# A hybrid SSM, attention and expert kernel: three PSUM banks for the up products and one for the attention

## The reference, cut to what matters

```
x = x + ssm(layernorm(x))        # scan over the tokens, 64 channels x 8 states
x = x + ffn(layernorm(x))        # 8 experts of 512, all computed, weighed by a router
x = x + attention(layernorm(x))  # 16 heads of 8; windows of 10 tokens with 25 to the left
x = x + ffn(layernorm(x))

g = einsum('bsh,ehf->ebsf', x, w_gate);  u = einsum('bsh,ehf->ebsf', x, w_up)
h = silu(g) * u
out = einsum('ebsh,bse->bsh', einsum('ebsf,efh->ebsh', h, w_down), cw)
```

## Time and profile before

| | |
|---|---|
| median of 3 runs | 1531.04 us (1530.69 to 1531.13) |
| the profiled execution | 1530.76 us, its span 1529.0 us |
| TensorE, its weight loads | 94%, 82% of the span |
| VectorE, ScalarE, GpSimd | 62%, 51%, 33% |
| granted TensorE clock, mean | 0.984 |

### The profile page before, as it was taken

How to read it: one execution, slowest core, us unless ns; L and a number is a source line. 1 busy time by engine, 2 the same in 40 slices (tenths; PEclk the granted TensorE clock), 3 DMA queues, 4 the chain that set the end, 5 groups by cost and what they waited for, 6 DMA issues and landing times.

```text
span 1529.0 us, 31357 instructions
## 1 busy us (share of the span) xinstructions
PE 1442.1 (94%) x12756; PEld 1247.8 (82%) x12756; DVE 946.7 (62%) x2125; ACT 772.8 (51%) x1037; POOL 503.1 (33%) x446
## 2 busy tenths in 40 slices
PE   5788889999999999999999989999999999999998
PEld 3677767888878878888888778888888888888887
DVE  5645558665766757666676566757765566575543
ACT  6453726654457444654546465455643554355321
POOL 5241344323432354135520373117511421241000
PEclk9999999999999999999999999999999999999999
DMA  5110151004201330024001510042004200420000
GB/s 184 33 48 23 45 143 32 19 27 131 40 2 41 105 81 2 9 89 116 14 2 39 134 43 13 1 136 57 29 2 118 40 2 1 118 40 1 2 7 8
DMA packets 82092, 75.50 MB, mean 49 GB/s; under 512 B 4748, under 2 KB 60076, under 8 KB 81948
## 3 DMA queue, kind: packets, MB, share of 16 engines
q1 hardware_dynamic: 74444, 58.58, 14.7%
q10 hardware_dynamic: 7504, 14.91, 2.7%
HBM read 60.65 MB, written 12.83 MB: 48 GB/s over the span
## 4 chain that ended last, share of the span: by engine, by line
PE 71%; DVE 9%; DMA 6%; ACT 5%; issue 5%; POOL 3%; SPq 1%; ACTq 0%; DVEq 0%; POOLq 0%
PE pd L1001 23%; PE pg L272 7%; PE pu L272 6%; PE pg L274 6%; PE pg L273 6%; PE pu L273 6%; PE pu L274 6%; DMA arena<-bc_spread 3%; PE att_ps L678 3%; DVE h L1094 2%; PE att_ps L700 2%; PE att_ps L705 1%; POOL arena L628 1%; DVE ffn_rows L295 1%; DMA qk_rows<-qk_parts 1%
## 5 line engine op out<-in xcount | busy, mean ns | idle before, releaser
L1056 ACT ACTIVATE h<-pg 128x512 f32<-128x512 f32 x512 | 303.4, 597 | 693.7 <-PE pg L274 687.5
L1001 PEld LDWEIGHTS pd<-w_down,h 128*128 128x128 f32 x4096 | 517.4, 194 | 31.9 <-issue 2.5
L1001 PE MATMUL pd<-w_down,h 128*128 128x128 f32 x4096 | 530.1, 278 | 0.8 <-DVE x L1082 0.8
L1094 DVE TENSOR_TENSOR h<-h,pu 128x512 f32<-128x512 f32 x512 | 345.6, 679 | 222.4 <-PE pu L274 220.7
L272 PE MATMUL pg<-ffn_x_hi,w_gate_hi 128*128 128x512 f32 x512 | 246.3, 481 | 1.5 <-DVE ffn_x_lo L355 1.5
L272 PE MATMUL pu<-ffn_x_hi,w_up_hi 128*128 128x512 f32 x512 | 207.0, 404 | 25.1 <-DVE h L1094 24.7
L273 PE MATMUL pg<-ffn_x_lo,w_gate_hi 128*128 128x512 f32 x512 | 204.6, 400 | 0.0
L274 PE MATMUL pg<-ffn_x_hi,w_gate_lo 128*128 128x512 f32 x512 | 204.4, 399 | 0.0
L273 PE MATMUL pu<-ffn_x_lo,w_up_hi 128*128 128x512 f32 x512 | 204.3, 399 | 0.0
L274 PE MATMUL pu<-ffn_x_hi,w_up_lo 128*128 128x512 f32 x512 | 204.2, 399 | 0.0
L903 POOL TENSOR_TENSOR att_arena<-att_arena 128x512 f32<-128x512 f32 (+1 forms) x72 | 72.8, 1011 | 349.4 <-DVE att_arena L775 349.2
(11 more groups left out here) (192 smaller groups left out, 1539.2 us busy)
## 6 DMA issues: line engine op xcount, KB each, us to landing
arena<-bc_spread ACTq DMA_DIRECT2D x56, 256.0 KB
att_arena<-v_rows SPq DMA_DIRECT2D x64, 144.0 KB, 3.9
qk_rows<-qk_parts SPq DMA_DIRECT2D x32, 256.0 KB, 3.1
q<-qk_rows SPq DMA_DIRECT2D x32, 256.0 KB, 3.7
k<-qk_rows SPq DMA_DIRECT2D x32, 256.0 KB, 4.5
att_arena<-v_rows SPq DMA_DIRECT2D x64, 128.0 KB, 3.6
arena<-in_x SPq DMA_DIRECT2D x8, 256.0 KB, 2.8
x<-in_x SPq DMA_DIRECT2D x8, 256.0 KB, 3.5
```

The costliest lines, as they stand in the source:

```text
L1001: last = nc.tensor.matmul(pd[:, t * P:(t + 1) * P], h_b[:, d % NH, t * P:(t + 1) * P], wd[:, d % NCH, :], start=d % CPE == 0 and t == 0, s ...
L1056: nc.scalar.activation(h_b[:, c % NH, :], pg[c % 2][:, :], ACT.Silu).then_inc(gate_done, 1)
L1094: nc.vector.tensor_tensor(h, h, pu[d % 2][:, :], ALU.mult).then_inc(h_done, 1)
```

## The change

The up products get a third bank: pu[d % 3], and the wait before up(d) is for h(d - 3) in place of h(d - 2). The bank is taken from the attention, whose att_ps then has one, with one pair of semaphores. In the setup of batch 0 the fourth b row uses pu[2] in place of att_ps[1]. With one bank each of ln3, q, k, v, s(n), o(n) and the projection must be read before the next may be written, and slots are moved: k from t0 + 6 (right behind q) to t0 + 7.5, its parts on ScalarE and VectorE and their stores on SP by 1.5 with it, v from t0 + 7.5 to t0 + 9, its copy from t0 + 8 to t0 + 9.5, the reloads of q and k from t0 + 8 to t0 + 9, v's store from t0 + 9 to t0 + 10, and o(n) from 3/8 to 1/2 of a unit.

```diff
--- before.py
+++ after.py
@@ -37,6 +37,7 @@
 SETUP = 40
 NXB = 4
 NH = 8
+NU = 3
 
 
 T_HEAD = [-4.5, 25] + [NCH * m - 8 for m in range(2, NM)]
@@ -178,9 +179,9 @@
         k3 = sb("k3", [P, 4, NKEY], F32R)
 
         pg = [ctx.enter_context(nc.psum_tensor(f"pg{i}", [P, L], F32)) for i in range(2)]
-        pu = [ctx.enter_context(nc.psum_tensor(f"pu{i}", [P, L], F32)) for i in range(2)]
+        pu = [ctx.enter_context(nc.psum_tensor(f"pu{i}", [P, L], F32)) for i in range(NU)]
         pd = ctx.enter_context(nc.psum_tensor("pd", [P, L], F32))
-        att_ps = [ctx.enter_context(nc.psum_tensor(f"att_ps{i}", [P, L], F32)) for i in range(2)]
+        att_ps = [ctx.enter_context(nc.psum_tensor("att_ps", [P, L], F32))]
         side_ps = [ctx.enter_context(nc.psum_tensor("side_ps", [P, L], F32))]
 
         packed, raw_loaded, stored = sem("packed"), sem("raw_loaded"), sem("stored")
@@ -193,7 +194,7 @@
         b_used, dx_done = sem("b_used"), sem("dx_done")
         g_full, u_full, gate_done, h_done = sem("g_full"), sem("u_full"), sem("gate_done"), sem("h_done")
         down_done, summed = sem("down_done"), sem("summed")
-        att_full, att_free = ([sem(f"att_{v}{i}") for i in range(2)] for v in ("full", "free"))
+        att_full, att_free = [sem("att_full")], [sem("att_free")]
         side_full, side_free = [sem("side_full")], [sem("side_free")]
         ln_sems = {k: (sem(f"{k}_stats"), sem(f"{k}_rstd"), sem(f"{k}_rows")) for k in ("ssm_ln", "att_ln", "ffn_ln")}
         fx_hi, fx_f32, route_exp, mix_ready = sem("fx_hi"), sem("fx_f32"), sem("route_exp"), sem("mix_ready")
@@ -266,7 +267,7 @@
         b = Banks(side_ps, side_full, side_free)
 
 
-        b_ps, c_ps = (pg[0], pg[1], pd, att_ps[1]), (pu[0], pu[1], att_ps[0], pg[0])
+        b_ps, c_ps = (pg[0], pg[1], pd, pu[2]), (pu[0], pu[1], att_ps[0], pg[0])
 
         def split3(out, w, x_parts, first=True, last=True):
             nc.tensor.matmul(out, w[0], x_parts[0], start=first, stop=False)
@@ -656,12 +657,12 @@
                 at, t0 = (lambda n: Att.at(j, n)), T_ATT[j]
                 yield t0 + 4
                 norm_pe(pe, ab, "att_ln", j, ("ln3", j), xn_att)
-                yield t0 + 6
-                ab.wait_free(pe, ("ln3", j))
                 for w, name in ((wq, ("q", j)), (wk, ("k", j))):
+                    yield t0 + (6 if w is wq else 7.5)
+                    ab.wait_free(pe, ("ln3", j))
                     ps = ab.take(pe, name)
                     ab.fill(split3(ps[:, :], [v[:, :] for v in w], (axh[:, 0:L], axl[:, 0:L])), name)
-                yield t0 + 7.5
+                yield t0 + 9
                 ps = ab.take(pe, ("v", j))
                 for t in range(TT):
                     out, xw = ps[:, t * P:(t + 1) * P], [a[:, t * P:(t + 1) * P] for a in (axh, axl)]
@@ -687,7 +688,7 @@
                     if n + 1 < NUNIT:
                         yield at(n + 1 + 1 / 8)
                         scores(n + 1)
-                    yield at(n + 1 + 3 / 8)
+                    yield at(n + 1 + 0.5)
                     if n in (0, NW // 4):
                         pe.wait_ge(v_set, 4 * j + (4 if n else 2))
                     name = ("o", j, n)
@@ -721,8 +722,8 @@
                 yield t0 + 4.5
                 ab.wait(act, ("ln3", j))
                 nc.scalar.copy(axh[:, 0:L], ab.ps(("ln3", j))[:, :]).then_inc(x_hi, 1)
-                yield t0 + 6.5
                 for w, v in enumerate("qk"):
+                    yield t0 + 6.5 + 1.5 * w
                     ab.wait(act, (v, j))
                     nc.scalar.activation(qk_s[:, w, 0, :], ab.ps((v, j))[:, :], ACT.Identity,
                                          bias=pk("b_" + v)).then_inc(qk_hi, 1)
@@ -744,12 +745,12 @@
                 dve.wait_ge(x_hi, j + 1)
                 ab.free(nc.vector.tensor_tensor(axl[:, 0:L], ab.ps(("ln3", j))[:, :], axh[:, 0:L].bitcast(F32),
                                                ALU.subtract), ("ln3", j))
-                yield t0 + 7
                 for w, v in enumerate("qk"):
+                    yield t0 + 7 + 1.5 * w
                     dve.wait_ge(qk_hi, 2 * j + w + 1)
                     ab.free(nc.vector.scalar_tensor_tensor(qk_s[:, w, 1, :], ab.ps((v, j))[:, :], pk("b_" + v),
                                                            qk_s[:, w, 0, :].bitcast(F32), ALU.add, ALU.subtract), (v, j))
-                yield t0 + 8
+                yield t0 + 9.5
                 ab.wait(dve, ("v", j))
                 if j == 0:
                     dve.wait_ge(v_pad, 32)
@@ -824,13 +825,13 @@
                     sp.wait_ge(qk_moved, 16 * 8 * (j - 1))
                 for w, v in enumerate("qk"):
                     for part in range(2):
-                        yield T_ATT[j] + 7 + 0.5 * w
+                        yield T_ATT[j] + 7 + 1.5 * w
                         if part == 0:
                             sp.wait_ge(qk_hi, 2 * j + w + 1)
                         else:
                             ab.wait_free(sp, (v, j))
                         sp.dma_start(qk_r[w, part], qk_s[:, w, part, :].bitcast(F32)).then_inc(qk_out[w][part], 16)
-                yield T_ATT[j] + 8
+                yield T_ATT[j] + 9
                 for w, (dst, parts) in enumerate(((q3, (0, 0, 1, 1)), (k3, (0, 1, 0, 1)))):
                     for i, part in enumerate(parts):
                         sp.wait_ge(qk_out[w][part], 16 * (j + 1))
@@ -838,7 +839,7 @@
                         sp.dma_start(dst[i::4, :, at0:at0 + L].bitcast(F32),
                                      qk_r[w, part].rearrange("(g e) l -> e g l", g=4)).then_inc(qk_moved, 16)
 
-                yield T_ATT[j] + 9
+                yield T_ATT[j] + 10
                 if j:
                     sp.wait_ge(v_moved[1], 16 * 8 * j)
                 ab.wait_free(sp, ("v", j))
@@ -987,9 +988,9 @@
                     d = c - 1
                     if 0 <= d < NC:
                         m = d // NCH
-                        if d >= 2:
-                            pe.wait_ge(h_done, d - 1)
-                        split3(pu[d % 2][:, :], [w[:, d % NCH, :] for w in wu],
+                        if d >= NU:
+                            pe.wait_ge(h_done, d - NU + 1)
+                        split3(pu[d % NU][:, :], [w[:, d % NCH, :] for w in wu],
                                (fxh[m % 2][:, :], fxl[m % 2][:, :])).then_inc(u_full, 1)
                     yield
                     for d in downs(c):
@@ -1091,7 +1092,7 @@
                         h = h_b[:, d % NH, :]
                         dve.wait_ge(gate_done, d + 1)
                         dve.wait_ge(u_full, d + 1)
-                        nc.vector.tensor_tensor(h, h, pu[d % 2][:, :], ALU.mult).then_inc(h_done, 1)
+                        nc.vector.tensor_tensor(h, h, pu[d % NU][:, :], ALU.mult).then_inc(h_done, 1)
                     d = c - 1 - LAG
                     if d >= 0 and d % CPE == CPE - 1:
                         weigh(d // CPE)
```

## The result

The changed kernel takes 1524.61 us (median of 6 runs, 1522.8 to 1526.8), the kernel before in the same runs 1530.43 us. The ratio is 0.9963 with a 95% interval of 0.9951 to 0.9976: faster by 5.8 us, a third of the 17.1 us that were forecast. The forecast's full range, 1503 to 1526, held it; the likeliest case's own range, 1507 to 1521, did not. A second measurement on another chip gave 1524.37 us and 0.9949 (0.9935 to 0.9962).

A forecast was written before the change was run, and what follows sets the result against it. TensorE, busy 1442.1 of 1529.0 us, was taken as the bound, so only its idle and slow-clock time could be won. Terms of -14.5, -5.1, -2, -2, +2, +2.5, +1.5, +0.5 gave -17.1: 1514 us, range 1503 to 1526.

The forecast's parts named there:

- the likeliest case: The forecast itself, not a rival: 1514 us, own range 1507 to 1521 us, chance 0.6.
- the two paced stretches: 76 to 125 and 160 to 215 us, where spread transfers set the pace: only about 2 us won in each.
- the end of the second paragraph: Up and down products: the third bank lets TensorE run one chunk further ahead of VectorE, not two; no size.
- isolated stalls, -14.5: Up's waits for h from 245 us on: about 16 us go, 1.5 us of the one at 547 us stays.
- Projections, +2 and +2.5: Moved k and v slots: +2 us of waits on VectorE, +2.5 us from later keys delaying scores(0), mainly batch 4.
- One attention bank, +1.5: o(n) waits for the mask addition to scores(n+1); its moved slot covers most of 8.0 us, leaving +1.5 us.
- SiLU, +0.5: Gate products that meet a late SiLU once the stall in front of them is gone: +0.5 us.
- Clock, -5.1: Half-clock stretches behind stalls at 714 and 1060 us are won, the one at 547 us is not: -5.1 us.
- All of it goes: Rival: stalls are a lack of banks everywhere, paced stretches too; some 1489 us, chance 0.1.
- slower by late keys: Rival: SP's reloads come so late that scores(0) waits across batches; 1549 us at 10 us later, chance 0.07.
- no difference: Rival: the stalls' time is VectorE's and reappears chunk by chunk; 1531 us, chance 0.06.
- The second, stalls that move: Rival: TensorE meets VectorE's lag at o or scores in the one attention bank; about 1527 or 1521 us, chance 0.17.

The follow-up runs named there:

- The cut spreads: Kernel before with each two-row spread transfer over 128 partitions cut into two of one row over 64: 1493.88 us, 0.9751; same cut in the changed kernel: 1486.15 us, 0.9708.

## Why the prediction came out as it did

**Accounts.** At the gate product of chunk 66 the changed kernel is 0.5 us behind (265.97 against 266.44 us), at that of chunk 67 0.4 us ahead, so of the -4 that was forecast for the two paced stretches nothing is left there. The forecast of -13.1 for the rest gave about -6 to -7 in the profiled run. Of this TensorE's busy time from 245 us on is 4.7 us: 1250.05 before, 1245.33 after.

```profile
245.00:1528.00 1283.00, 1250.05 (x11698) 1090.51 (x11696) 802.84 (x1808) 649.68 (x870) 407.98 (x358) 0.99 0.16 44
```

```profile
245.00:1528.00 1283.00, 1245.33 (x11701) 1086.91 (x11699) 801.21 (x1809) 650.05 (x870) 408.14 (x358) 0.99 0.16 44
```

The clock thus gave about what was forecast for it (5.1). The idle terms (-14.5, +4.5, +1.5, +0.5, together -8) gave some -1 to -2; the waits named above sum to -1.3.

**The step that failed** is the end of the second paragraph: "So the third bank lets TensorE run one chunk further ahead of VectorE and not two: after it the down products and the up product wait for the same thing." It counts the down products' wait for h and leaves out the other one: each expert's first down product (L1002) waits for `summed`, VectorE's read of pd by the weighing of the expert before (L1083). The code has it: the first down product of expert e is issued in chunk 4e + 5, behind up(4e + 4), and the weighing it needs stands in VectorE's queue directly behind h(4e + 2), the very multiply that this up product needed with two banks. For one chunk in four there was thus hardly any room to win. The term "isolated stalls, -14.5" measured -10.1 of up (by the weight loads' count 19.0 - 3.1 = 15.9) and +5.4 of pd (by theirs 8.7 - 1.4 = 7.3): -5 to -9. The row that tells it stood in the view that was read, as a wait of pd of 0.6 us from 245 us on: small, most likely because up waited ahead of it.

Place by place the timelines of TensorE bear this out. Of the ten up waits from 245 us on, those in chunks 68, 148, 196, 207 and 356, together 4.0 us, are gone without a trace. The other five come back as waits of pd, each in the next chunk of the form 4e + 5 (its own, where it has that form): 0.59 us in chunk 97 as 0.56 in chunk 97, 2.42 in 222 as 1.64 in 225, 1.37 in 289 as 0.99 in 289, 1.43 in 340 as 0.80 in 341, and the 2.88 of chunk 164 as 2.64 of up and 1.36 of pd in 165. The second profile of the changed kernel has pd waits in the same five chunks (and splits the one in 225 over 225 and 229).

The stall at 547 us, the longest, shows it in rows. TensorE and VectorE of the changed kernel:

```profile
549.78 0.50 PE L273 MATMUL pu<-ffn_x_hi,w_up_hi 128*128 128x512 f32 x1 [2.64 <-DVE h L1095]
...
552.10 3.75 PE L1002 MATMUL pd<-w_down,h 128*128 128x128 f32 x16 [1.36 <-DVE x L1083]
```

```profile
545.73 1.44 DVE L582 SCALAR_TENSOR_TENSOR arena<-arena 128x512 f32<-128x512 f32 x1 [7.18 <-POOL arena L631]
...
549.07 0.65 DVE L1095 TENSOR_TENSOR h<-h,pu 128x512 f32<-128x512 f32 x1
...
550.84 1.11 DVE L1083 SCALAR_TENSOR_TENSOR x<-pd,mix,x 128x128 f32<-128x128 f32 x4
```

The forecast was 1.5 us of the 2.88 of the earlier trace rows. It is 2.64 of up and, right behind it, 1.36 of pd. TensorE got its chunk more of room and used it up, because VectorE's own scan came later: the multiply on GpSimd that it waits for started at 544.34 us, behind the landing of its spread, and in the kernel before at 541.59. In the changed kernel v's eight reloads are issued from 537.64 us, before that from 540.01. But the scan is as late without them. In the second profile of the changed kernel v's reloads are issued from 542.71 us, the up wait is 2.25 us and the pd wait again 1.36, and the multiply does not wait for its spread at all. It stands in GpSimd's queue behind the first query products, which wait for k's reload:

```profile
539.52 2.04 POOL L884 TENSOR_TENSOR q_weights<-q,pack 128x512 fp32r<-128x512 f32 x2 [10.80 <-DMA k<-qk_rows]
...
543.64 1.26 POOL L631 TENSOR_TENSOR arena<-arena 128x512 f32<-128x512 f32 x1
```

With v later it is the same (539.51 and 543.62 us, an up wait of 1.70). So the multiply starts late behind a transfer each time, once the spread and twice k's reload, and which of them it is differs between two runs of one kernel. The gate product of chunk 168, at 557.85 us before, starts 4.1 us later in the changed kernel (1.6 us of it are older than this stall), and only by chunk 228, at 734 us, are the two level again: there the changed kernel has no stall at 714.

**Paced stretches, -2 each: nothing left of it.** The spreads stayed 5.35 us apart ((122.25 - 84.86) / 7 = 5.34), as argued, and up(22) did start when up(21) had: 120.91 us, where the earlier trace rows have 120.44 and 122.83. Of this gain two thirds were lost right behind it. The product itself and the down products behind it in the changed kernel:

```profile
120.91 0.80 PE L273 MATMUL pu<-ffn_x_hi,w_up_hi 128*128 128x512 f32 x1 [3.35 <-DVE h L1095]
...
122.36 1.89 PE L1002 MATMUL pd<-w_down,h 128*128 128x128 f32 x8
```

TensorE had come a chunk further and waited longer for the same multiply, 3.35 us in place of 1.95, and behind it the granted clock falls to 1.2 GHz: eight down products take 1.89 us (1.06 before), and the mean of 119 to 124 us is 0.67, where it was 1.00. The second profile has the same, 3.34 us and 0.66. "a longer single stall may cost clock" was in the text, at 0.4 us; from up(22) to the next gate product it is 5.26 us in place of 3.68, so it cost 1.6 of the 2.4. Earlier in the stretch the clock went the other way, which was not forecast: from 98 to 114 us, where the kernel before has 0.79 behind waits of 2.23 and 1.99 us, the changed one has 1.00 with up waits of 0.83 and 1.66 us. TensorE's waits for VectorE in this stretch did not fall: 6.2 us of up and 0.2 of pd before, 5.8 of up and 1.6 of pd after. In the second stretch k waited until 194.36 us (forecast 194.48):

```profile
194.36 0.77 PE L273 MATMUL att_ps<-attn_x,w_k_hi 128*128 128x512 f32 x1 [6.54 <-DVE qk_parts L751]
...
208.21 2.65 PE L1002 MATMUL pd<-w_down,h 128*128 128x128 f32 x16 [1.99 <-DVE x L1083]
```

but then pd waited 1.99 us at 208.21, and up(49) came at 211.93 and not at 210.2 us. Here too the missing step is pd's bank. The 1.1 us by which the changed kernel is ahead at the gate products of chunks 51 to 55 are lost at 228 to 231 us, where its transposes into the side bank wait 2.1 us for VectorE (1.3 before), with the granted clock at 0.83 from 225 to 235 us (1.00 before); in the second profile they are lost by chunk 60.

**Projections, +2 and +2.5.** v and k wait +1.7 us from 245 us on: right. The late keys did not appear: before scores(0) of batch 4 the wait fell from 3.03 to 0.57 us, since GpSimd's first query product started at 857.18 and not at 860.05 us, though SP issued k's reloads 0.7 us later. Their landing is set by other traffic, as was noted, but it moved to the better. In their place the late part is o(0) of that batch, put at 0: it waits 7.16 us in place of 4.65.

```profile
859.37 1.05 PE L679 MATMUL att_ps<-k,q_weights 128*128 128x64 f32 x8 [0.57 <-POOL q_weights L884]
...
881.81 0.44 PE L701 MATMUL att_ps<-attn_p_t,att_arena 128*32 128x32 f32 x16 [7.16 <-POOL att_arena L892]
```

It still starts 2 us earlier than before (883.86): TensorE reaches it earlier than the heads gain.

**One attention bank, +1.5, and SiLU, +0.5.** No wait for the mask addition is left, and 1.3 us of one for the SiLU. At its old slot o waited 10.2 us, where 8.0 was reckoned. Right in mechanism, 1.5 too high.

**Clock, -5.1: about -5, in part by luck.** At 714 and 1062 us it is full, as said:

```profile
713.00:722.00 9.00, 8.67 (x119) 7.75 (x118) 8.14 (x14) 5.41 (x8) 5.27 (x4) 1.00 0.46 99
1061.00:1067.00 6.00, 6.00 (x97) 5.23 (x96) 3.45 (x7) 4.07 (x5) 3.58 (x3) 1.00 0.01 3
```

But (1 - clock) times the length also fell by 3.2 us from 855 to 895 us (0.83 to 0.91), behind the wait of scores(0), and by 1.6 from 420 to 440, which was not forecast; and it rose by 3.4 us from 520 to 560, behind the stall at 547 us and ahead of it, and by 1.7 from 1335 to 1350. The sum over all six places is about 17 us before and about 12 after, in both profiles of the changed kernel, though the shares of the places differ between them. The two places that were forecast gave their 5.1; the four others nearly cancel, and that is luck.

**Rivals.** "All of it goes", "slower by late keys" and "no difference" did not happen. The second, stalls that move, was right that VectorE's lag isn't shortened and its stalls come back elsewhere (1521 to 1527 held the result), and wrong about where: not in the attention bank, which with two up banks costs nothing measurable, but in pd's, and, where pd's was eased, in the side bank. Its time fits for a reason that is only half its own, and the range reaches beyond 1521 us for its sake alone: that it held the result is luck as far as the likeliest case goes.

The share of 0.12 of the DMA engines was read as a reason for the pace and not as something to change. The Trainium skill, "DMA: Bandwidth & Descriptors", Rules for kernel authors, names this very case, an outermost dimension of less than 16, and its remedy, to put a dimension whose size is a multiple of 16 outermost. The cut spreads agree: with a broadcast over 64 partitions outermost the share goes to 0.52 while they run, the same multiplies no longer wait for a transfer, and 2.5% of the time goes without any other bank.

## What to carry to other kernels

Before giving a bank to a queue that waits, list every wait that stands within one slot behind it on the same engine, and compare which read of the slower engine each needs: the gain is the room up to the next of them, not the wait that is shown. Then look at what makes the slower engine late: here the shape of one transfer did so in two stretches and in batch 4's attention, and mending it was worth 2.5%, the third bank 0.2 to 0.4%, and after the cut 0.7%. The two are not the same remedy, since the cut left 11.0 of 12.7 us of the isolated stalls. And a chunk of lead that is won in front of a paced input is waited off at the next one: a wait of 1.95 us became 3.35 us, and half clock behind it took 1.6 of the 2.4 us back.

## What the runs showed of the hardware unexpectedly

A multiply-add of 128x128 on VectorE took 426 ns with its first operand in SBUF and 344 ns with it in PSUM, 512 times each. Two transfers of one row over 64 partitions, issued one after the other, landed in 2.9 us each (median) at a DMA share of 0.52 and before GpSimd asked for them, where one transfer of both rows kept a multiply waiting every 5.35 us at a share of 0.13. Where TensorE's half clock falls differs from run to run of the same kernel: in the changed one the granted clock from 1340 to 1347 us was 0.76 in one profile and 1.00 in the other, at spans of 1522.8 and 1522.7 us.
